# A graph kernel's first stage: x loaded by the block, four one-hot places, fewer sign passes

## What is computed

```python
deg_out = jnp.clip(segment_sum(ones, src, num_segments=n), 1.0)
deg_in = jnp.clip(segment_sum(ones, dst, num_segments=n), 1.0)
h = feats * rsqrt(deg_out)[:, None]
m = segment_sum(h[src], dst, num_segments=n) * rsqrt(deg_in)[:, None]
x = m @ W_gc + b_gc + (feats @ W_res + b_res)
core = _moe_ff(x, Wg, bg, w1, b1, w2, b2)        # top 2 of 64 experts
y = x + core
z = (y - mean(y, 0)) * rsqrt(var(y, 0) + eps) * gamma + beta
out = _layernorm(feats + z)
```

## Time and profile before

| | us |
|---|---|
| median of 3 runs | 1657.07 (1651.96 to 1659.29) |
| the profiled execution | 1655.46 |
| its span, first to last instruction | 1653.6 |
| TensorE busy | 1483.0 (90%) |
| VectorE busy | 1096.2 (66%) |
| ScalarE busy | 697.4 (42%) |
| GpSimd busy | 469.6 (28%) |
| mean granted clock | 0.957 |

### The profile page before, as it was taken

One profiled execution on the slowest core, in us unless ns is written; L12 is line 12 of the kernel. 1 busy time (PEld: TensorE's weight loads), 2 busy tenths in 40 slices (PEclk: granted clock), 3 DMA queues, 4 the chain that ended last, 5 costly groups with the idle time before them and its releaser, 6 DMA issues.

```text
span 1653.6 us, 42138 instructions
## 1 busy us (share of the span) xinstructions
PE 1483.0 (90%) x11682; PEld 1253.0 (76%) x11683; DVE 1096.2 (66%) x2604; ACT 697.4 (42%) x1610; POOL 469.6 (28%) x442
## 2 busy tenths in 40 slices
PE   5988858999999999999999997699999999999662
PEld 4866747877777787777777786688888888888562
DVE  6976898787788788788778775344444444444377
ACT  1647765443434344434443442233333333333257
POOL 4356100112112112111111212455555555555100
PEclk9998979999999999999999998799999999999785
DMA  9212110101101101101101022786667856763594
GB/s 295 80 61 60 58 37 10 43 14 39 51 13 38 51 13 38 51 13 38 37 27 38 20 71 71 230 271 224 214 218 247 270 178 226 251 215 97 186 301 151
DMA packets 146095, 188.11 MB, mean 114 GB/s; under 512 B 16117, under 2 KB 114200, under 8 KB 145763
## 3 DMA queue, kind: packets, MB, share of 16 engines
q1 hardware_dynamic: 126034, 150.59, 27.8%
q0 software_dynamic: 18144, 35.99, 6.8%
q10 hardware_dynamic: 1872, 1.02, 0.2%
HBM read 141.42 MB, written 51.21 MB: 116 GB/s over the span
## 4 chain that ended last, share of the span: by engine, by line
PE 76%; DVE 6%; issue 5%; ACT 4%; DMA 2%; another core or an unknown queue 2%; DVEq 2%; SPq 1%; POOL 0%; ACTq 0%; POOLq 0%
PE banks L1070 32%; PE banks L1176 13%; PE banks L1185 12%; PE banks L1058 9%; PE banks L974 4%; DVE work L1282 3%; PE banks L955 2%; PE banks L1162 1%; ACT counts_r L803 1%; PE banks L1089 1%; DMA big<-ytab 1%; SPq L571 1%; DVE stats L1738 1%; PE banks L1079 1%
## 5 line engine op out<-in xcount | busy, mean ns | idle before, releaser
L1070 PE MATMUL banks<-parts_r,counts_r 128*128 128x512 f32 x2401 | 609.0, 401 | 13.6 <-ACT counts_r L803 12.6
L1070 PEld LDWEIGHTS banks<-parts_r,counts_r 128*128 128x128 f32 x2401 | 437.1, 189 | 107.2 <-issue 22.3
L803 ACT CAST counts_r<-banks 128x784 fp32r<-128x784 f32 x392 | 301.8, 816 | 445.1 <-PE banks L1058 426.4
L1282 DVE TENSOR_TENSOR work<-edge,iota_two 128x1024 bf16<-128x1024 bf16 (+1 forms) x784 | 435.9, 622 | 47.5 <-PE banks L1058 36.0
L637 POOL DMA_INDIRECT lists<-entry,slot x98 | 120.1, 1225 | 735.4 <-DVEq L1541 661.3
L1176 PE MATMUL banks<-work 128*128 128x128 f32 x1984 | 250.9, 280 | 11.7 <-ACT work L862 4.1
L1176 PEld LDWEIGHTS banks<-work 128*128 128x128 f32 x1984 | 233.6, 193 | 25.2 <-issue 17.0
L1185 PE MATMUL banks<-big,work 128*128 x992 | 234.7, 380 | 1.5 <-ACT work L873 1.5
L1652 DVE COPY work<-work 128x1024 f32 x125 | 94.7, 757 | 184.9 <-PE banks L1176 101.3
L1058 PEld LDWEIGHTS banks<-work 128*128 128x128 bf16 x3136 | 152.8, 98 | 71.8 <-issue 70.4
L1058 PE MATMUL banks<-work 128*128 128x98 bf16 x3136 | 184.8, 210 | 17.8 <-DVE work L1282 9.0
(11 more groups left out here) (219 smaller groups left out, 1182.6 us busy)
## 6 DMA issues: line engine op xcount, KB each, us to landing
work<-in_L_gnn_w_dram SPq DMA_DIRECT2D x64, 512.0 KB
big<-in_L_gnn_w_dram SPq DMA_DIRECT2D x64, 512.0 KB
ytab<-zeros SPq DMA_DIRECT2D x11, 1024.0 KB
big<-in_L_gnn_b_dram SPq DMA_DIRECT2D x64, 128.0 KB
restab<-big SPq DMA_DIRECT2D x7, 896.0 KB, 4.0
big<-xtab SPq DMA_DIRECT2D x7, 896.0 KB
res_mem<-restab SPq DMA_DIRECT2D x24, 256.0 KB, 2.9
xtab<-pair_mem SPq DMA_DIRECT2D x24, 256.0 KB, 2.2
```

The lines of the kernel that those rows point to most:

```text
L803: nc.scalar.copy(counts[h][:, :, i * WB * WN:(i + 1) * WB * WN].rearrange("p b (h w) -> p h b w", h=2), built_ps[i % 2][:, :, 0:WB * WV // ...
L1070: last = pe.matmul(agg_ps[h], counts[h][:, b, :], parts[:, b, :], start=(b == 0), stop=(b == NB - 1))
L1282: return dve.tensor_tensor(hot, digits.rearrange("p (c t) -> p c t", t=2).unsqueeze(2).to_broadcast([P, c, n, 2]), iota_two[:, 0:n, :].uns ...
```

## The change

Five edits in stage A.

1. **x by the block.** The three loads into `G` go. SP loads each block of 128 rows from DRAM into one of two buffers `feats[b % 2]` as soon as the transposes of block b - 2 are done, and TensorE transposes from there. ScalarE's `stage_feats` goes. The stores to `restab` are placed in SP's list between the loads; the store of product blocks 0 to 6 stands behind the load of block 10, and so on every seven.
2. **Four places.** Two more one-hot places lie where `src_i` and `digit_i` were. `hist_used` starts at 4. VectorE's loop bodies have four counts, with odd pairs written out; TensorE's first six counts are written out.
3. **Two sign passes per tile** instead of three in `count_window`.
4. **Three joint passes.** After tiles 8, 17 and 24 one sign pass with a sum runs over `rel_w` of nine, nine and seven tiles. It stands for the sums of the pass that went; the test for the general path has a new constant.
5. **Digits.** `hi_w` moves to the array `edge`, and VectorE makes the high and low digits ahead of its wait for the window counts.

The diff, cut to its core:

```diff
-        hist_lo = [part(AW + s * HB1, HB1).bitcast(BF16).rearrange("p (c v t) -> p c v t", v=LO, t=2) for s in range(2)]
-        hist_wide = [part(AW + 2 * HB1 + s * HB2, HB2).bitcast(BF16) for s in range(2)]
+        HB = HB1 + HB2
+        hist_at = [AW, AW + HB, 0, HB]
+        hist_lo = [part(at, HB1).bitcast(BF16).rearrange("p (c v t) -> p c v t", v=LO, t=2) for at in hist_at]
+        hist_wide = [part(at + HB1, HB2).bitcast(BF16) for at in hist_at]
...
-        hi_w = part(0, NWT * P).bitcast(I32).rearrange("p (t c) -> p t c", t=NWT)
+        hi_w = edge[:, :].bitcast(I32).rearrange("p (t c) -> p t c", t=NWT)
...
@@ SP @@
-            sp.dma_start(G[:, 0:FIRST, D:2 * D], blocks(x, 0, FIRST)).then_inc(feats_first, 16)
+            for b in range(2):
+                sp.dma_start(feats[b], x[b * P:(b + 1) * P, :]).then_inc(feats_in[b], 16)
             pad_ends(1, src, src_flat)
-            sp.dma_start(G[:, FIRST:NB - 1, D:2 * D], blocks(x, FIRST, NB - 1 - FIRST)).then_inc(feats_in, 16)
-            sp.dma_start(G[0:TAIL, NB - 1, D:2 * D], x[(NB - 1) * P:N, :]).then_inc(feats_in, 16)
...
-            for j in range(NPC):
+            def store_res(j):
                 sp.wait_ge(prod_copied, (j + 1) * BLK7 + 2)
                 sp.dma_start(blocks(restab, j * BLK7, BLK7), G[:, j * BLK7:(j + 1) * BLK7, D:2 * D]).then_inc(res_out[j // LATE], 16)
+
+            for b in range(2, NB):
+                rows = P if b < NB - 1 else TAIL
+                sp.wait_ge(fT_summed, b - 1)
+                sp.dma_start(feats[b % 2][0:rows, :], x[b * P:b * P + rows, :]).then_inc(feats_in[b % 2], 16)
+                if b == NB - 1:
+                    sp.wait_ge(consts, 1)
+                    sp.dma_start(feats[b % 2][TAIL:P, :], zeros[TAIL:P, :]).then_inc(feats_in[b % 2], 16)
+                if b > BLK7 and (b - 3) % BLK7 == 0:
+                    store_res((b - 3) // BLK7 - 1)
+            store_res(NPC - 1)
...
@@ ScalarE @@
-            def stage_feats(b):
-                if not isinstance(b, int) or b > 0:
-                    act.wait_ge(fT_summed, b)
-                nc.scalar.copy(fblk, G[:, ds(b, 1), D:2 * D].rearrange("p b d -> p (b d)")).then_inc(f_staged, 1)
...
-                for m in range(3):
-                    count_below(spare[:, m * P:(m + 1) * P], tile, below[:, m, ds(t, 1)], signs[:, 2 + m, ds(t, 1)])
+                for m in range(2):
+                    count_below(spare[:, m * P:(m + 1) * P], tile, below[:, 1 + m, ds(t, 1)], signs[:, 3 + m, ds(t, 1)])
                 nc.scalar.activation(rel_w[:, t, :], tile, ACT.Identity, bias=first_n[:, t:t + 1], scale=float(NB))
+                if t % NTB == NTB - 1 or t == NWT - 1:
+                    c = t // NTB
+                    n = t + 1 - c * NTB
+                    act.drain()
+                    nc.scalar.activation(spare[:, 0:n * P], rel_w[:, c * NTB:t + 1, :].rearrange("p t c -> p (t c)"), ACT.Sign,
+                                         bias=eps_c[:, :], scale=1.0, accum_out=signs[:, 2, c:c + 1])
...
@@ TensorE @@
-            pe.sem_inc(hist_used, 2)
+            pe.sem_inc(hist_used, 4)
...
-                pe.wait_ge(f_staged, b + 1)
+                pe.wait_ge(feats_in[s], loaded)
                 for k in range(K):
-                    m = pe.transpose(fT_ps[:, k, :], fblk[:, k * P:(k + 1) * P], ident[:, :])
+                    m = pe.transpose(fT_ps[:, k, :], feats[s][:, k * P:(k + 1) * P], ident[:, :])
...
@@ VectorE @@
+            for s in range(2, 4):
+                dve.memset(hist_wide[s][:, HC * HI:], 0.0)
+            dve.drain()
...
             def count_pairs(first, end):
-                with dve.Fori(first, end) as i:
-                    for s in range(2):
-                        count(i * 2 + s, s)
+                a, z = first + first % 2, end - end % 2
+                for g in range(2 * first, 2 * a):
+                    count(g, g % 4)
+                if z > a:
+                    with dve.Fori(a // 2, z // 2) as i:
+                        for s in range(4):
+                            count(i * 4 + s, s)
+                for g in range(2 * max(z, a), 2 * end):
+                    count(g, g % 4)
...
-            dve.wait_ge(window_counted, 1)
             dve.wait_ge(src_w_in, 16 * NWT)
+            dve.wait_ge(lists_out, 16)
             dve.tensor_scalar(hi_w, src_w, P.bit_length() - 1, None, ALU.logical_shift_right)
             dve.drain()
             dve.scalar_tensor_tensor(low_w, hi_w, float(-P), src_w, ALU.mult, ALU.add)
+            dve.wait_ge(window_counted, 1)
             dve.tensor_tensor(rel_w, rel_w, hi_w, ALU.add)
```

More of the change, by code:

```diff
@@ L152, in gnn_kernel @@
         pick = part(A1, 4 * P).rearrange("p (m n) -> p m n", m=4)
-        spare = part(A1 + 4 * P, 3 * P // 2).bitcast(BF16)
+        NTB = -(-NWT // 3)
+        spare = part(A1 + 4 * P, NTB * P // 2).bitcast(BF16)
         A2 = AW - NWT * ROW
@@ L250, in gnn_kernel @@
         pair_x = [pair_mem[:, s * 2 * D:(s + 1) * 2 * D].rearrange("p (b d) -> p b d", b=2) for s in range(2)]
-        fblk = pair_mem[:, 0:D]
+        feats = [pair_mem[:, s * D:(s + 1) * D] for s in range(2)]
+        fblk = feats[0]
         bias_x = pair_mem[:, 2 * D:4 * D].rearrange("p (m d) -> p m d", m=2)
@@ L717, in feats_step @@
                     turn_feats(b + 1, 1 - s)
-                if not isinstance(b, int) or b + 2 < NB:
-                    stage_feats(b + 2)
             def share(b, first, n):
                 return range((b - first) * NWT // n, (b - first + 1) * NWT // n)
-            act.wait_ge(feats_first, 16)
-            stage_feats(0)
             turn_feats(0, 0)
-            stage_feats(1)
-            for b in range(FIRST - 2):
+            for b in range(2):
                 feats_step(b, b % 2)
-            act.wait_ge(feats_in, 32)
-            with act.Fori(FIRST // 2 - 1, B_FOUND[0] // 2) as i:
+            with act.Fori(1, B_FOUND[0] // 2) as i:
                 for s in range(2):
@@ L975, in multiply, with feats_total, feats_step @@
                 last.then_inc(multiplied, 1)
-            def feats_step(b, s, pair=None):
-                if not isinstance(b, int) or b + 1 < NB:
-                    turn_feats(b + 1)
+            def feats_total(b):
+                return 16 * (b // 2 + 1) + (16 if b == NB - 1 else 0)
+            def feats_step(b, s, pair=None, i=None, at=0):
+                if i is not None:
+                    turn_feats(b + 1, 1 - s, i * 16 + 16 * (s + 1))
+                elif b + 1 < NB:
+                    turn_feats(b + 1, 1 - s, feats_total(b + 1))
                 if pair is not None:
-                    count(pair * 2, 0)
+                    count(pair * 2, at)
                 multiply(b, s)
                 if pair is not None:
-                    count(pair * 2 + 1, 1)
+                    count(pair * 2 + 1, at + 1)
             def turn_digits(t):
@@ L1005, in _ @@
             pe.matmul(hist_ps, zeros[:, 0:P], zeros[:, 0:LO], start=True, stop=False, skip_group_check=True)
-            with pe.Fori(0, LEAD) as i:
-                for s in range(2):
-                    count(i * 2 + s, s)
+            for g in range(2 * LEAD):
+                count(g, g % 4)
             pe.wait_ge(weights_in, NW)
-            turn_feats(0)
+            turn_feats(0, 0, feats_total(0))
             with pe.Fori(0, (G_DIGITS - LEAD) // 2) as i:
                 for s in range(2):
-                    feats_step(i * 2 + s, s, i * 2 + (s + LEAD))
+                    feats_step(i * 2 + s, s, i * 2 + (s + LEAD), i, (s + LEAD) % 2 * 2)
             for b in range(G_DIGITS - LEAD, B_DIGITS):
@@ L1376, in _ @@
             count_pairs(G_DEG, NHG // 2)
-            count(NHG - 1, 0)
+            count(NHG - 1, (NHG - 1) % 4)
             is_general = dve.value_load(general[0:1, 0:1], min_val=0, max_val=1)
```

30 lines of the change are left out of this document (17 added, 13 removed).

## The result

The changed kernel takes **1671.26 us** (median of 4, 1667.12 to 1673.83) against 1654.51 us (median of 4) for the kernel before in the same comparison: ratio **1.010**, 95% interval 1.0072 to 1.0128. I had forecast 1630 us, 1620 to 1648, with a chance of 0.08 for slower. It is slower by 17 us (1%), clear of the interval.

The account below looks back on a forecast made before the run. Stage A was held bound by VectorE and TensorE waiting for each other over two places. Its end 26.9 us earlier, less 1.7 us for the clock, gave 25.2 us off 1655.46: 1630 us, range 1620 to 1648.

Parts of the forecast that it names:

- They wait for each other in turn, as two partners do that share only two buffers.: Stage A, VectorE and TensorE: their mutual waits, 28.6 and 24.4 us, were put down to having only two one-hot places.
- whatever delays the release: Stage A, 95 to 176 us: ten late releases of 1.7 to 3.2 us stall VectorE and TensorE with two places.
- Start, gathers, windows: Stage A: start gains 5.2 us, gathers 1.49 us apart land at 163.1, ScalarE's window steps fall to 2.6 us.
- rival (c): Stage A: block loads of x late at every block, total 1685 us; chance 0.05.
- rival (d): Stage A: GpSimd's gathers starve beside a VectorE without holes, stage ends 55 us later, total 1710 us; chance 0.03.
- ScalarE in the windows: Stage A, steps 22 to 39: ScalarE needs about 3.3 us a step, 2.6 after the change, so no longer a bound.
- The sum for stage A: 25.2 us: Stage A: closing matmul at 198.4 us, 26.9 us earlier, less 1.7 us for the clock, gives 25.2 us gained.
- the 0.84 us a step: Stage A, steps 1 to 40: 3.86 us a step would fall to TensorE's own 3.02, 39 steps taking 117.8 us.
- Rival (a): Stage A: late releases stay on the path through ScalarE's copies, 12 us lost again, total 1642 us; chance 0.20.
- (e): Stage A: little moves, window wait and late releases eat all but a few us, 1650 to 1660 us; chance 0.07.
- Everything after the stage as long as before, 1653.6 - 226 or some 1428 us.: After stage A: a sign to check, all later stages unchanged at some 1428 us.

Follow-up runs that it names:

- f3: Kernel before with four one-hot places instead of two, nothing else, chip 4: 1612.02 us, ratio 1.0029 to the kernel before.
- f1: Kernel before, unchanged, run again on chip 4: 1608.59 us, one run.
- f2: Changed kernel, unchanged, run again on chip 4: 1632.50 us, ratio 1.0156 to the kernel before.
- h2: Kernel before, unchanged, on chip 10: 1608.49 us, one run.
- h1: Changed kernel with 86 empty drains on ScalarE and 133 on TensorE, on chip 10: 1600.47 us, ratio 0.9949 to the kernel before.
- g2: Kernel before with 123 empty drains on TensorE at its start, chip 0: 1616.05 us, ratio 1.0057 to the kernel before.
- g3: Changed kernel with 60 empty drains on ScalarE, chip 0: 1607.52 us, one run.
- g4: Changed kernel with 128 empty drains on ScalarE, chip 0: 1631.80 us, one run.
- g1: Changed kernel with 86 empty drains on ScalarE and 133 on TensorE, chip 0: 1598.93 us, ratio 0.9951 to the kernel before.
- e2: Kernel before with 170 empty drains on ScalarE at its start, chip 15: 1632.45 us, ratio 1.0147 to the kernel before.
- e3: Changed kernel with 30 empty drains on ScalarE, chip 15: 1664.64 us, ratio 1.0339 to the kernel before.
- e1: Changed kernel with 86 empty drains on ScalarE, chip 15: 1609.36 us, ratio 1.0006 to the kernel before.

## Why the prediction was wrong

Five steps, in its order.

**"They wait for each other in turn, as two partners do that share only two buffers."** Half right: f3, with only the places changed, gains 6.7 us. But the size was read from one profiled execution: 3.86 us a step and ten waits of 1.7 to 3.2 us. In f1 the same kernel opens step 1 at 35.82 and step 40 at 165.15 us, 3.32 us a step, and f2 opens them at 36.56 and 157.40, 3.10. The room over TensorE's own 3.02 was 0.3 us a step, not 0.84. The earlier trace rows held the sign: a count ended at 130.96 and VectorE went on at 134.99. I wrote "whatever delays the release" and costed four places as if they could hide it. Nothing in the code explains 4 us between an increment and its waiter; that should have been an unknown of its own, with zero gain as one end.

**Start, gathers, windows.** On the chip without stops the picture of the *changed* kernel was close. f2's timelines, the successors of L1335 and L1357, and its two waits:

```profile
84.49 0.17 DVE L1357 TENSOR_SCALAR signs<-row_w 128x25 f32<-128x25 int32 x1
```

```profile
162.39 1.83 DVE L1379 TENSOR_SCALAR edge<-work 128x3200 int32<-128x3200 int32 x1 [6.95 <-DMA work<-srcpad,edge_w]
```

```profile
DVE edge L1379 <- DMA work<-srcpad,edge_w: 6.9, 1, 6.9
...
ACT work L708 <- DMA work<-dstpad,edge_w: 4.1, 1, 4.1
...
PE banks L975 <- DMA pair_mem<-in_x_dram: 1.0, 1, 1.0
```

I had the edge list at 86.0, the digits at 163.1 after a wait for a DMA, a wait of ScalarE of some 6 us for a gather, and the end of the stage at 198.4; measured 84.49, 162.39, 4.1 and 197.16. TensorE waits 1.0 us in all for x, so rival (c) is out, and rival (d) with it: the gathers keep some 1.49 us. (In (c) a step without counts would cost 4.3 - 1.95 = 2.35 us more and not 2.1, which changes nothing.) Where it went wrong is the difference. The kernel before has its edge list at 87.38 and its digits at 167.99 us there: 2.9 us are gained at the start, not 5.2, and 5.6 at the digits, not 26.

**ScalarE in the windows.** "Without this part of the change it would be the next one." Right for the digits, and worth little. The kernel before (f1) and f3, which keep three sign passes and staging, start their digits after a wait for ScalarE's window counts (the first and second row), where f2 waits for the gathers:

```profile
167.99 1.83 DVE L1357 TENSOR_SCALAR work<-work 128x3200 int32<-128x3200 int32 x1 [2.04 <-ACTq L762]
```

```profile
163.87 1.83 DVE L1368 TENSOR_SCALAR edge<-work 128x3200 int32<-128x3200 int32 x1 [5.11 <-ACTq L764]
```

So with four places ScalarE is the next bound, by 1.5 us (163.87 against 162.39), and the stage ends 0.5 us later (197.66 against 197.16). A joint pass took 1.26 us, where I had 1.3.

**The sum for stage A: 25.2 us.** Measured 7.2 (f1 to f2), 7.3 on chip 10 (h2 to h1), 9.1 to 9.6 on chip 0 (g2 to g3, g4 and g1), and 1.3 in the first comparison. The term that was mis-sized is the 0.84 us a step, 33 us over 39 steps; the steps had 0.3 us to give. Rival (a), late releases stay on the path, and (e), little moves, came nearest for stage A, but I gave both less room than their evidence deserved.

**"Everything after the stage as long as before, 1653.6 - 226 or some 1428 us."** This is the step that turned the sign. It was 1447.8 us, 19.9 more. I had no rival for it: I had priced the instructions that went and came in stage A, and not that they stand ahead of later loops. On chip 4 the loss is 31.1 us in the experts. (In the first comparison it is 18.7: the kernel before took 6.9 us more there than in f1 and the changed one 5.5 less than in f2, which I can't explain.) The parts add up: 24.4 for ScalarE's loop (e2 on the kernel before) and 5.8 or 6.3 for TensorE's (f3, g2), 30.2 to 30.7. With 7.2 us gained, 0.9 more in the edge sum and 1.0 in the rest it comes to 25.8; the medians differ by 25.4. In the profile shown before the change nothing pointed to it except the page's line of queue 14, 26 packets of 0.20 MB in all. Its trace has none between 1110 and 1540 us: the expert loop stays loaded, and so could cease to.

## What to carry to other kernels

An edit that changes the number of instructions ahead of a hot loop can change that loop: look at the instruction queues' packets inside it, before and after, and if they rise, put empty instructions where the engine idles, and time the edit only then. Here the same edit was 1.6% slower or 0.5% faster than the kernel before, by 86 and 133 drains. And before a wait in one trace is taken as what an edit can win, it should have a reason in the code; a release that arrives 4 us after its increment has none, and was gone in the next trace of the same kernel.

## What the runs showed of the hardware that I had not expected

- ScalarE's loop of 316 instructions stays loaded or is fetched again in each pass by where it begins, with a period of 128 as far as one bad place shows it: 25 to 27 packets in an execution, or 102 to 103, and nothing between. The cost of a bad place was 24 us at 24 modulo 128 (e2 against f1) and some 58 us at 54 (e3 against e1's 486.3 us), over 480 us of loop.
- TensorE stopped once for 3.9 to 5.8 us, near the entry of its loop, in all ten runs with its code moved by 123 instructions and in none of the seven others, with a 16 KB packet of queue 8 starting within each stop; DMA ran at 373 GB/s during g2's. In the first comparison's changed kernel the stop of 5.21 us ended at 1087.73 us.
- One kernel, unchanged, took 1648 to 1659 us in the first comparison and 1604 to 1611 us on four chips, with a mean granted clock of 0.957 and 0.960 in the profiled executions (the first trace and f1). The difference lay in waits, and hardly in the length of instructions: between 250 and 1000 us TensorE waited 12.6 us for ScalarE's L803 in the first and not at all for the same line in e2, while the edge sum's matmul (L1070) had a mean of 401 and 398 ns.
